# Two graph layers on one core: the filter's first products of two quads issued as a pair, projection and filter 2 in one PSUM bank

## Chip, cores and metric

The kernel runs on one core of one Trainium2 chip. The metric is device time in microseconds (us); before the change the median of three runs is 1879.74 us (1878.91 to 1882.81).

## What is computed

50,000 nodes and 50,000 edges, 128 channels, f32 in and out. A SchNet-like layer (senders `src`, receivers `dst`) is followed by a layer with a mean over neighbours (gather by `dst`, sum by `src`); each has a layer norm and a relu in front. The edges are sorted by `dst`. Cut to what matters:

```python
h = relu(layernorm(x))                                   # per node
basis = exp(-coef * (edge_weight[:, None] - centers)**2) # 50 centres per edge
ef = (softplus(basis @ Wf1 + bf1) - LOG2) @ Wf2 + bf2    # the filter, per edge
messages = (h @ W_lin.T)[src] * ef
agg = segment_sum(messages, dst)
x = x + (softplus(agg @ Wm1 + bm1) - LOG2) @ Wm2 + bm2
h = relu(layernorm(x))
neigh = h[dst] @ W_neigh.T + b_neigh
x = x + h @ W_self.T + b_self + segment_sum(neigh, src) / clip(count, 1)
```

## The kernel before, in words

The rows are handled in quads of 512 (four tiles of 128), 98 of them. The program has three parts: a sorting part (counts and ranks of the indices), one long software-pipelined part, and a final part that sums rows by bins (L1262 and around it). The change touches only the middle part.

The middle part is a sequence of steps s = 0 to 115, written out by `over_steps`: every engine runs its own `step(s, ...)`, and in step s it works on quads of several ages: quad s at the front of the pipeline, quad s-18 at its end. `there(q)` leaves out quads that don't exist. Order on one engine is program order; between engines there are semaphores that count quads (`pe.wait_ge(e_hT, s - 2 + 1)` waits until hT of quad s-2 is written). Most buffers exist once, some twice.

On the edge side a quad passes through these stations. GpSimd gathers its `x` rows (L787). VectorE takes row statistics (L819, L826), ScalarE and VectorE make the inverse root between them, ScalarE normalises (`norm_relu`, L1021, output xn). TensorE transposes xn into turn_ps (`turn`, L1097), ScalarE copies it out as hT, and TensorE multiplies it by wlin into proj_ps (`product`, L1091: the projection). Beside this, ScalarE makes the basis of two quads at a time (`make_basis`, L989 and L993, in even steps): partitions 0 to 49 hold that of the even quad, partitions 64 to 113 that of the odd one. TensorE multiplies one of the halves by wf1 into u_ps (`filter_up`, L1104), ScalarE and VectorE form the softplus (`clamp` L998, `exponential` L1002, `logarithm` L1007, `soften` L859; the result is su), and TensorE multiplies su by wf2 into filt_ps (L1091, after a bias product L1089: filter 2). ScalarE copies this out as efs (`evacuate`, L1027; the trace calls it efb), and VectorE multiplies proj_ps by efs (`message`, L870, counted by e_msg).

On the node side TensorE sums message windows (`block_sums`, L1113, 12 products of 64 rows in alternating halves of the array), ScalarE copies the sums out (aggs), TensorE multiplies by wm1 (L1150, into nu_ps) and later by wm2 ("mlp"), VectorE adds the residual (L897), normalises (L890), TensorE transposes (L1097 with comb), ScalarE copies out nhT, and TensorE forms `self` (wself) and `neigh` (wneigh). `hidden_out` (L1033) is ScalarE's copy of `neigh` to h1s; it waits for n_neigh. `edge_rows` (L1125) gathers rows of a stored h1 by one-hot products, and `rows_out` (L1040) copies them out.

What sets the order of the work is the text of each engine's step. Before the change TensorE's step s is: self(s-11), block_sums(s-8), mlp(s-9), edge_rows(s-17), wm1(s-8), filter_up(s), neigh(s-11), transpose of nxn(s-10), projection(s-2), filter 2(s-1), transpose of xn(s-1). ScalarE's step s is: aggs(s-9), hT(s-3), efs(s-3), norm_relu(s-2), clamp(s-9), rows_out(s-18), hidden_out(s-12), nhT(s-11), small logarithms and roots, exponential and logarithm (s-9), clamp and exponential (s-1), in even steps make_basis, logarithm(s-1). VectorE's step s is: one_hots(s-8), edge_hots(s-17), message(s-3), small work and soften(s-9), node_out(s-11), small work, node_norm(s-10), soften(s-1), residual(s-9), row statistics.

Of PSUM's eight banks the middle part names u_ps (0), turn_ps (1), proj_ps (2), filt_ps (3), two banks of tiles (4, 5), nu_ps (6) and node_ps (7).

Of the kernel before, what the change touches and what calls it, by code (L numbers as in the profile page):

```python
# [17 lines left out]
BASIS = 50  # L18
BASIS_AT = (0, 64)
# [132 lines left out]
def gnn_kernel(nc, ins, out_dram):  # L152
# [5 lines left out]
    with ExitStack() as ctx:  # L158
# [456 lines left out]
        with nc.If(unfit == 0), ExitStack() as fast:  # L615
# [9 lines left out]
            with ExitStack() as sems:  # L625
# [37 lines left out]
                x_keys, x_win, scattered = sa2("x_keys"), sa2("x_win"), sa2("scattered")  # L663
                x_hot, x_sum, x_src, x_pos, x_rows = sa("x_hot"), sa("x_sum"), sa("x_src"), sa("x_pos"), sa("x_rows")
                x_ones = sa("x_ones")
                u_ps, turn_ps, proj_ps, filt_ps, _, _, nu_ps, node_ps = bank
                self_ps = mlp_ps = neigh_ps = node_ps
                agg_at, rows_at = 0, 2 * P

# [143 lines left out]
                def _(dve):  # L813
# [106 lines left out]
                    def step(s, even, odd, pair, slot, late):  # L920
                        if there(s - 8):
                            one_hots(s - 8, even)
                        if there(s - 17):
                            edge_hots(s - 17, odd)
                        if there(s - 3):
                            message(s - 3, odd)
                        if there(s - 10):
                            square_root(s - 10, nroot, nsquare, n_root, n_square)
                        if there(s - 1):
                            square_root(s - 1, root[:], square[:], e_root, e_square)  # L930
                        if there(s - 10):
                            times_var(s - 10, nmv, nsquare, nratio, n_square, n_ratio)
                        if there(s - 2):
                            dst_column(s - 2, even)
                        if there(s - 1):
                            times_var(s - 1, emv[:, odd, :, :], square[:], ratio[:], e_square, e_ratio)
                        if there(s - 9):
                            soften(s - 9, nu_ps[:], bm1_low, nlu[:], nsu[:], n_softln, n_mlp, n_soft)
                        if there(s - 10):
                            correction(s - 10, nratio, nfactor, n_ratio, n_factor)  # L940
                        if there(s - 1):
                            correction(s - 1, ratio[:], factor[:], e_ratio, e_factor)
                        if there(s - 11):
                            node_out(s - 11, odd, late)
                        if there(s - 17):
                            row_keys(s - 17, odd)
                        if there(s - 1):
                            inverse_root(s - 1, factor[:], root[:], rstd[:], e_factor, e_norm, e_rstd)
                        if there(s - 10):
                            inverse_root(s - 10, nfactor, nroot, nrstd, n_factor, None, n_rstd)  # L950
                        if there(s - 7):
                            window_dst(s - 7, odd)
                        if there(s - 10):
                            node_norm(s - 10, even)
                        if there(s - 1):
                            mean_shift(s - 1, emv[:, odd, :, :], rstd[:], shift[:], e_rstd, e_shift)
                            soften(s - 1, u_ps[:], bf1_low, ln_out[:], su[:], e_softln, e_filter, e_soft)
                        if there(s - 9):
                            residual(s - 9, odd)
                        if there(s):  # L960
                            dve.wait_ge(gathered[even], half_count(s, even, 64))
                            row_stats(xg[:, even, :, :], stats, e_stats)
                            if there(s + 2):
                                take_src(s + 2, even)
                        if there(s - 9):
                            dve.wait_ge(n_x1, s - 9 + 1)
                            row_stats(x1[:, odd, :, :], nstats, n_stats)
                        if there(s):
                            wait_used(dve, e_ln, s, 2)
                            row_aggr(s, stats, emv[:, even, :, :], e_stats, e_aggr)  # L970
                        if there(s - 9):

                            wait_used(dve, n_ln, s - 9, 1)
                            row_aggr(s - 9, nstats, nmv, n_stats, n_aggr)
# [7 lines left out]
                def _(act):  # L982
# [58 lines left out]

                    nc.scalar.preload_act_table_set("natural_log_exp_and_others")
                    def step(s, even, odd, pair, slot, late):
                        if there(s - 9):
                            evacuate(s - 9, by_half(aggs[:]), tiles_ps(agg_at), n_agg, n_u, n_aggT)
                        if there(s - 3):
                            evacuate(s - 3, hT[:], turn_ps[:], e_turned, e_proj, e_hT)
                            evacuate(s - 3, efs[:], filt_ps[:], e_filter, e_msg, e_filter_sb)
                        if there(s - 2):
                            act.wait_ge(e_shift, s - 2 + 1)  # L1050
                            wait_used(act, e_turned, s - 2, 1)
                            norm_relu(xg[:, even, :, :], rstd, shift, xn, e_norm)
# [18 lines left out]
                        if there(s - 9):  # L1071
                            logarithm(s - 9, neu[:], nlu[:], n_exp, n_soft, n_softln)
                        if there(s - 1):
                            clamp(s - 1, u_ps[:], bf1_top, clampu[:], e_u, e_clamp)
                            exponential(s - 1, clampu[:], eu[:], e_clamp, e_exp)
                        if even == 0 and there(s):
                            make_basis(pair, slot)
# [5 lines left out]
                def _(pe):  # L1083
# [13 lines left out]
                            last = nc.tensor.transpose(turn_ps[:, t * P:(t + 1) * P], source[:, t, :], ident[:])  # L1097
                        last.then_inc(done, 1)

                    def filter_up(q, par, pair, slot):  # L1100
                        pe.wait_ge(basis_ready, pair + 1)
                        wait_used(pe, e_soft, q, 1)
                        at = BASIS_AT[par]
                        nc.tensor.matmul(u_ps[:], wf1[at:at + BASIS, :], basis[at:at + BASIS, slot, :], start=True, stop=True).then_inc(e_u, 1)  # L1104

                    def block_sums(j, par):
                        pe.wait_ge(n_hot, j + 1)
# [21 lines left out]
                    def step(s, even, odd, pair, slot, late):  # L1129
# [5 lines left out]
                        if there(s - 8):  # L1135
                            if there(s - 18):
                                pe.wait_ge(x_rows, s - 18 + 1)
                            block_sums(s - 8, even)
                        if there(s - 9):
                            if there(s - 11):  # L1140
                                pe.wait_ge(n_y, s - 11 + 1)
# [5 lines left out]
                        if there(s - 8):  # L1147
                            pe.wait_ge(n_aggT, s - 8 + 1)
                            wait_used(pe, n_soft, s - 8, 1)
                            nc.tensor.matmul(nu_ps[:], wm1[:], aggs[:], start=True, stop=True).then_inc(n_u, 1)  # L1150
                        if there(s):
                            filter_up(s, even, pair, slot)
                        if there(s - 11):
                            pe.wait_ge(n_y, s - 11 + 1)
                            if there(s - 9):
# [2 lines left out]
                        if there(s - 10):  # L1158
# [3 lines left out]
                                pe.wait_ge(e_hT, s - 2 + 1)  # L1162
                            wait_used(pe, n_hT, s - 10, 1)
                            turn(nxn, n_turned)
                        if there(s - 2):
                            product(s - 2, proj_ps, hT, wlin, None, e_hT, e_msg, e_proj)
                        if there(s - 1):
                            product(s - 1, filt_ps, su, wf2, 0, e_soft, e_filter_sb, e_filter)
                            pe.wait_ge(e_norm, s - 1 + 1)

# [990 lines left out]
```

## Time and profile before

| what | value |
|---|---|
| median of 3 runs | 1879.74 us (1878.91 to 1882.81) |
| profiled execution, its own time | 1883.8 us |
| its span in the profile | 1882.0 us |
| TensorE busy | 1690.9 us, 90% |
| VectorE busy | 1418.4 us, 75% |
| ScalarE busy | 1133.3 us, 60% |
| GpSimd busy | 1119.4 us, 59% |
| mean granted TensorE clock | 0.947 |

The profile shows one execution. The busy time of an engine is the union of its instructions' times, so that overlapping matmuls count once; of a matmul the end is modelled, so the distance from one group's start to the next one's is the safer measure of what it costs. An f32 product shows as two matmul records, each with its weight load: four products of 128 columns are "x8". In a timeline a row gives the start in us from the start of the span, the duration in us, engine, line, operation, names and shapes, and in brackets how long the engine sat idle before and who ended that. An instruction's start already has its semaphore waits behind it.

### The profile page before, as it was taken

How to read it: one execution, taken by the hardware profiler on the slowest of the kernel's cores; microseconds unless marked ns; L12 is line 12 of the kernel's file. 1: busy time of each engine (PE TensorE's matmuls, PEld its weight loads, DVE VectorE, ACT ScalarE, POOL GpSimd, SP SyncE). 2: the span in 40 equal slices, each digit the busy share in tenths (PEclk: the TensorE clock that was granted, in tenths of full speed). 3: DMA queues.
4: the chain of work that ended last, by engine and by line, in shares of the span. 5: the costliest groups of instructions: out<-in, count | busy, mean ns of one | idle time of the engine just before them, and what ended most of it. 6: DMA issues, size and time to landing. Idle time of an engine off the chain costs nothing. (4 is left out here: it accounts for less than half of the span.)

```text
span 1882.0 us, 49986 instructions
## 1 busy us (share of the span) xinstructions
PE 1690.9 (90%) x13254; PEld 1271.4 (68%) x13254; DVE 1418.4 (75%) x4622; ACT 1133.3 (60%) x2713; POOL 1119.4 (59%) x938
## 2 busy tenths in 40 slices
PE   2659679999999999999999999999999738888997
PEld 1223256777777777777777777777777628888897
DVE  8989647877787778777877777777777517777886
ACT  1007678877777777777777777777774303333333
POOL 5980144366666666666666666666653545566675
PEclk8769769999999999999999999999999859999999
DMA  2000035667777777777777766666666538999886
GB/s 81 0 0 1 23 94 141 177 202 209 217 211 206 207 212 215 207 206 213 212 204 206 208 196 185 187 193 190 184 177 184 144 107 254 265 272 269 244 224 171
DMA packets 293579, 333.96 MB, mean 177 GB/s; under 512 B 42220, under 2 KB 233710, under 8 KB 293486
## 3 DMA queue, kind: packets, MB, share of 16 engines
q1 hardware_dynamic: 216654, 255.35, 47.1%
q0 software_dynamic: 25088, 51.83, 10.0%
q10 hardware_dynamic: 51744, 25.70, 4.6%
q8 instruction: 39, 0.64, 0.2%
q14 instruction: 54, 0.44, 0.1%
HBM read 212.96 MB, written 119.75 MB: 177 GB/s over the span
## 5 line engine op out<-in xcount | busy, mean ns | idle before, releaser
L787 POOL DMA_INDIRECT xg<-in_x,srcs x392 | 418.6, 1068 | 423.4 <-issue 348.5
L798 POOL DMA_INDIRECT row_table<-row_out,posq x392 | 384.4, 981 | 174.3 <-issue 113.2
L1262 PE MATMUL psum<-bin_rows,bin_hot 128*128 128x129 f32 x2352 | 288.9, 281 | 53.7 <-DVE bin_hot L1235 53.5
L1262 PEld LDWEIGHTS psum<-bin_rows,bin_hot 128*128 128x128 f32 x2352 | 273.0, 193 | 69.7 <-DVE bin_hot L1235 40.3
L1235 DVE TENSOR_TENSOR bin_hot<-iota,bin_rel 128x1536 f32<-128x1536 f32 x98 | 176.6, 1802 | 5.3
L1125 PE MATMUL psum<-hwin,hotT 64*128 64x128 f32 x2352 | 166.5, 291 | 14.3 <-DMA hwin<-h_table 11.2
L870 DVE TENSOR_TENSOR msgw<-psum,efb 128x512 f32<-128x512 f32 x98 | 67.7, 691 | 147.2 <-PE psum L1091 117.9
L1125 PEld LDWEIGHTS psum<-hwin,hotT 64*128 64x128 f32 x2352 | 147.2, 197 | 26.9 <-issue 9.4
L1113 PE MATMUL psum<-hot,win 64*128 64x128 f32 x2352 | 159.3, 282 | 2.4 <-DVE hot L882 2.4
L1021 ACT ACTIVATE xn<-xg,shift,rstd 128x128 f32<-128x128 f32 x392 | 161.0, 494 | 0.0
L1089 PE MATMUL psum<-bias,ones 3*128 3x512 bf16 x392 | 152.1, 388 | 7.9 <-ACT h1s L1033 6.4
L1113 PEld LDWEIGHTS psum<-hot,win 64*128 64x128 f32 x2352 | 140.4, 189 | 14.6 <-DVE hot L882 2.6
L1104 PE MATMUL psum<-basis,wf 50*128 50x512 f32 x196 | 115.6, 671 | 25.8 <-DVE su L859 19.6
L1277 ACT ACTIVATE x<-psum,inverse 128x128 f32<-128x128 f32 x200 | 57.2, 368 | 128.6 <-DVE inverse L1245 128.6
L1033 ACT ACTIVATE h1s<-psum 128x512 f32<-128x512 f32 x98 | 58.6, 598 | 124.0 <-PE psum L1091 94.6
L569 ACT ACTIVATE psum<-psum,cols 128x196 f32<-128x196 f32 x130 | 51.1, 393 | 127.9 <-PE psum L544 127.9
L998 ACT ACTIVATE nclamp<-psum,cols 128x512 f32<-128x512 f32 x98 | 67.4, 688 | 94.8 <-PE psum L1150 94.0
L1089 PEld LDWEIGHTS psum<-bias,ones 3*128 3x128 bf16 x392 | 35.5, 91 | 122.9 <-issue 89.8
L1091 PE MATMUL psum<-wf,su 128*128 128x128 f32 x784 | 118.1, 296 | 0.0
L1277 ACT ACTIVATE nx<-psum,inverse 128x128 f32<-128x128 f32 x192 | 54.9, 369 | 102.2 <-DVE inverse L1245 102.2
L1091 PEld LDWEIGHTS psum<-wf,su 128*128 128x128 f32 x784 | 98.9, 198 | 23.3 <-issue 23.3
L1091 PE MATMUL psum<-wneigh,nhT 128*128 128x128 f32 x784 | 114.0, 288 | 0.0
(174 smaller groups left out, 3870.8 us busy)
## 6 DMA issues: line engine op xcount, KB each, us to landing
bin_rows<-row_table SPq DMA_DIRECT2D x196, 195.0 KB, 3.2
win<-msg_table SPq DMA_DIRECT2D x392, 96.8 KB
hwin<-h_table SPq DMA_DIRECT2D x392, 96.0 KB
msg_table<-msgw SPq DMA_DIRECT2D x98, 258.0 KB
nx<-in_x_nodes SPq DMA_DIRECT2D x98, 256.0 KB
h_table<-h1s SPq DMA_DIRECT2D x98, 256.0 KB
y_table<-ys SPq DMA_DIRECT2D x61, 256.0 KB
out<-xg ACTq DMA_DIRECT2D x50, 256.0 KB, 3.8
```

The source lines that it names most:

```text
L787: nc.gpsimd.indirect_dma_start(out=xg[:, par, t, :], out_offset=None, in_=ins["x"], in_offset=bass.IndirectOffsetOnAxis(ap=srcs[:, par, t: ...
L798: nc.gpsimd.indirect_dma_start(out=row_dram, out_offset=bass.IndirectOffsetOnAxis(ap=posq[:, par, t:t + 1], axis=0), in_=row_out[:, par, t ...
L870: nc.vector.tensor_tensor(msgw[:, par, :, 0:C], proj_ps[:].rearrange("p (t c) -> p t c", t=QT), efs[:].rearrange("p (t c) -> p t c", t=QT) ...
L1021: last = nc.scalar.activation(out[:, t, :], source[:, t, :], ACT.Relu, bias=shift_[:, t:t + 1], scale=rstd_[:, t:t + 1])
L1089: nc.tensor.matmul(ps[:], ones3[0:3, :], bias3[0:3, b, :], start=True, stop=False)
L1091: last = nc.tensor.matmul(ps[:, t * P:(t + 1) * P], left[:, t * P:(t + 1) * P], weights_[:], start=(b is None), stop=(b is None or t == QT ...
L1104: nc.tensor.matmul(u_ps[:], wf1[at:at + BASIS, :], basis[at:at + BASIS, slot, :], start=True, stop=True).then_inc(e_u, 1)
L1113: last = nc.tensor.matmul(tile_ps(agg_at, 2 * g + h), win[half_of(h), par, g, w, 0:C], hot[half_of(h), par, g, w, :], start=(w == 0), stop ...
L1125: last = nc.tensor.matmul(tile_ps(rows_at, 2 * g + h), hotT[half_of(h), par, g, w, :], hwin[half_of(h), par, g, w, :], start=(w == 0), sto ...
L1235: nc.vector.tensor_tensor(bin_hot[:, par, :, :, :], iota4[:].rearrange("p (b n) -> p b n", b=2).unsqueeze(2).broadcast_to([P, 2, BTILES, B ...
L1262: last = nc.tensor.matmul(bank[2 * slot + b][:, h * MW:(h + 1) * MW], bin_hot[:, slot % 2, b, w, h * P:(h + 1) * P], bin_rows[:, slot, b, ...
L1277: last = nc.scalar.activation(of_slot(means, slot)[:, t, :], sums_of(slot)[:, t // 2, t % 2, 0:C], ACT.Identity, scale=inverse[:, slot, t ...
```

## The change

`filter_up` is called in even steps only, and then issues the products of both quads of the pair, one behind the other: the even quad's from partitions 0 to 49 into bank 0, the odd one's from partitions 64 to 113 into bank 3. Filter 2 no longer has bank 3 and shares bank 2 with the projection. So TensorE's projection of quad s-2 moves from behind the nxn transpose to directly behind `block_sums`, and first waits until ScalarE has copied out filter 2 of the same quad; filter 2 of quad s-1 first waits for the message of quad s-2. On ScalarE the copies hT(s-3) and efs(s-3) move ahead of aggs(s-9).

```diff
-                u_ps, turn_ps, proj_ps, filt_ps, _, _, nu_ps, node_ps = bank
+                u_even, turn_ps, edge_ps, u_odd, _, _, nu_ps, node_ps = bank
+                u_of = (u_even, u_odd)
+                proj_ps = filt_ps = edge_ps
...
-                            soften(s - 1, u_ps[:], bf1_low, ln_out[:], su[:], e_softln, e_filter, e_soft)
+                            soften(s - 1, u_of[odd][:], bf1_low, ln_out[:], su[:], e_softln, e_filter, e_soft)
...
-                        if there(s - 9):
-                            evacuate(s - 9, by_half(aggs[:]), tiles_ps(agg_at), n_agg, n_u, n_aggT)
                         if there(s - 3):
                             evacuate(s - 3, hT[:], turn_ps[:], e_turned, e_proj, e_hT)
                             evacuate(s - 3, efs[:], filt_ps[:], e_filter, e_msg, e_filter_sb)
+                        if there(s - 9):
+                            evacuate(s - 9, by_half(aggs[:]), tiles_ps(agg_at), n_agg, n_u, n_aggT)
...
-                            clamp(s - 1, u_ps[:], bf1_top, clampu[:], e_u, e_clamp)
+                            clamp(s - 1, u_of[odd][:], bf1_top, clampu[:], e_u, e_clamp)
...
-                    def filter_up(q, par, pair, slot):
+                    def filter_up(q, pair, slot):
+
                         pe.wait_ge(basis_ready, pair + 1)
                         wait_used(pe, e_soft, q, 1)
-                        at = BASIS_AT[par]
-                        nc.tensor.matmul(u_ps[:], wf1[at:at + BASIS, :], basis[at:at + BASIS, slot, :], start=True, stop=True).then_inc(e_u, 1)
+                        for par, at in enumerate(BASIS_AT):
+                            nc.tensor.matmul(u_of[par][:], wf1[at:at + BASIS, :], basis[at:at + BASIS, slot, :], start=True, stop=True).then_inc(e_u, 1)
...
                             block_sums(s - 8, even)
+                        if there(s - 2):
+                            pe.wait_ge(e_filter_sb, s - 2 + 1)
+                            product(s - 2, proj_ps, hT, wlin, None, e_hT, e_msg, e_proj)
...
-                        if there(s):
-                            filter_up(s, even, pair, slot)
+                        if even == 0 and there(s):
+                            filter_up(s, pair, slot)
...
-                        if there(s - 2):
-                            product(s - 2, proj_ps, hT, wlin, None, e_hT, e_msg, e_proj)
                         if there(s - 1):
+                            wait_used(pe, e_msg, s - 1, 1)
                             product(s - 1, filt_ps, su, wf2, 0, e_soft, e_filter_sb, e_filter)
```

On TensorE, one step of the middle part, from block_sums (hot, win) to the transpose of xn. Before, every step reads:

```order
L1113 MATMUL psum<-hot,win 128x128 x12
L1089 MATMUL psum<-bias,ones 128x512
L1091 MATMUL psum<-wm,nsu 128x128 x4
L1125 MATMUL psum<-hwin,hotT 128x128 x12
L1150 MATMUL psum<-aggs,wm 128x512
L1104 MATMUL psum<-basis,wf 128x512
L1089 MATMUL psum<-bias,ones 128x512
L1091 MATMUL psum<-wneigh,nhT 128x128 x4
L1097 MATMUL psum<-ident,comb 128x128 x4
L1091 MATMUL psum<-wlin,hT 128x128 x4
L1089 MATMUL psum<-bias,ones 128x512
L1091 MATMUL psum<-wf,su 128x128 x4
```

Now an even step reads as below; an odd step is the same without the row of the basis (L1107).

```order
L1116 MATMUL psum<-hot,win 128x128 x12
L1093 MATMUL psum<-wlin,hT 128x128 x4
L1091 MATMUL psum<-bias,ones 128x512
L1093 MATMUL psum<-wm,nsu 128x128 x4
L1128 MATMUL psum<-hwin,hotT 128x128 x12
L1156 MATMUL psum<-aggs,wm 128x512
L1107 MATMUL psum<-basis,wf 128x512 x2
L1091 MATMUL psum<-bias,ones 128x512
L1093 MATMUL psum<-wneigh,nhT 128x128 x4
L1099 MATMUL psum<-ident,comb 128x128 x4
L1091 MATMUL psum<-bias,ones 128x512
L1093 MATMUL psum<-wf,su 128x128 x4
```

The projection (wlin, hT) stands four products earlier, ahead of mlp, edge_rows, wm1 and neigh, and the basis product is there twice in one step and not in the next.

On ScalarE, the end of one step and the start of the next. Before (lu is the logarithm of the edge side):

```order
L1007 ACTIVATE lu<-eu,cols 128x512
L1025 REGISTER_ALU
L1027 ACTIVATE aggs<-psum 128x2x2x128
L1027 ACTIVATE hT<-psum 128x512
L1027 ACTIVATE efb<-psum 128x512
L1021 ACTIVATE xn<-xg,shift,rstd 128x128 x4
```

Now:

```order
L1009 ACTIVATE lu<-eu,cols 128x512
L1029 ACTIVATE hT<-psum 128x512
L1029 ACTIVATE efb<-psum 128x512
L1027 REGISTER_ALU
L1029 ACTIVATE aggs<-psum 128x2x2x128
L1023 ACTIVATE xn<-xg,shift,rstd 128x128 x4
```

The copy of filter 2 (efb) is now the second behind the logarithm, where it was the third.

## Rows read from the trace of the kernel before

**Rows 1.** The page: its first line and the engines' busy time

```profile
span 1882.0 us, 49986 instructions
PE 1690.9 (90%) x13254; PEld 1271.4 (68%) x13254; DVE 1418.4 (75%) x4622; ACT 1133.3 (60%) x2713; POOL 1119.4 (59%) x938
```

**Rows 2.** Two stretches: length, busy PE PEld DVE ACT POOL, clock, DMA share, GB/s

```profile
500.00:600.00 100.00, 100.00 (x832) 75.03 (x832) 78.05 (x327) 77.31 (x168) 66.19 (x64) 1.00 0.73 210
1600.00:1700.00 100.00, 86.67 (x703) 81.82 (x701) 74.95 (x117) 33.16 (x116) 61.76 (x30) 0.98 0.93 269
```

**Rows 3.** Timeline of TensorE, one step and what leads into it

```profile
804.24 0.60 PE L1097 MATMUL psum<-ident,comb 128*128 128x128 f32 x4
804.68 1.06 PE L1091 MATMUL psum<-wlin,hT 128*128 128x128 f32 x8
805.67 0.38 PE L1089 MATMUL psum<-bias,ones 3*128 3x512 bf16 x1
...
806.98 0.60 PE L1097 MATMUL psum<-ident,xn 128*128 128x128 f32 x4
807.51 0.39 PE L1089 MATMUL psum<-bias,ones 3*128 3x512 bf16 x1
...
808.91 1.61 PE L1113 MATMUL psum<-hot,win 64*128 64x128 f32 x24
810.45 0.38 PE L1089 MATMUL psum<-bias,ones 3*128 3x512 bf16 x1
...
811.86 1.61 PE L1125 MATMUL psum<-hwin,hotT 64*128 64x128 f32 x24
813.39 1.13 PE L1150 MATMUL psum<-aggs,wm 128*128 128x512 f32 x2
814.45 1.12 PE L1104 MATMUL psum<-basis,wf 50*128 50x512 f32 x2
815.50 0.39 PE L1089 MATMUL psum<-bias,ones 3*128 3x512 bf16 x1
...
816.82 0.60 PE L1097 MATMUL psum<-ident,comb 128*128 128x128 f32 x4
```

**Rows 4.** Timeline of ScalarE, an odd step's and an even step's second half

```profile
804.52 0.60 ACT L1033 ACTIVATE h1s<-psum 128x512 f32<-128x512 f32 x1 [1.36 <-PE psum L1091]
...
808.75 0.72 ACT L1007 ACTIVATE lu<-eu,cols 128x512 f32<-128x512 f32 x1
...
817.10 0.60 ACT L1033 ACTIVATE h1s<-psum 128x512 f32<-128x512 f32 x1 [1.36 <-PE psum L1091]
...
822.02 0.63 ACT L993 ACTIVATE basis<-junk 128x512 f32<-128x512 f32 x1
822.55 0.71 ACT L1007 ACTIVATE lu<-eu,cols 128x512 f32<-128x512 f32 x1
823.17 0.58 ACT L1027 ACTIVATE aggs<-psum 128x512 f32<-128x512 f32 x1
823.64 0.59 ACT L1027 ACTIVATE hT<-psum 128x512 f32<-128x512 f32 x1
```

**Rows 5.** Timeline of all engines where TensorE waits for a ScalarE copy

```profile
289.01 0.60 ACT L1027 ACTIVATE aggs<-psum 128x512 f32<-128x512 f32 x1 [1.86 <-PE psum L1113]
...
289.66 1.12 PE L1150 MATMUL psum<-aggs,wm 128*128 128x512 f32 x2 [0.70 <-ACT aggs L1027]
```

**Rows 6.** Timeline of VectorE, from the residual to the message

```profile
812.02 0.69 DVE L897 TENSOR_TENSOR x<-psum,nx 128x512 f32<-128x512 f32 x1
...
816.01 0.95 DVE L910 TENSOR_TENSOR hotT<-dst_keys,reach 128x768 f32<-128x768 int32 x1
818.35 0.69 DVE L870 TENSOR_TENSOR msgw<-psum,efb 128x512 f32<-128x512 f32 x1 [1.39 <-PE psum L1091]
```

**Rows 7.** Line L1113, the first 80 ns of one block_sums: ns min/median/max, starts

```profile
L1113 PE MATMUL psum<-hot,win x2: 373/373/373, 821.5 to 821.5; 64*128 64x128 f32 x2
```

**Rows 8.** Timeline of TensorE behind a longer idle time, early in the middle part

```profile
304.94 2.93 PE L1113 MATMUL psum<-hot,win 64*128 64x128 f32 x24 [2.38 <-DVE hot L882]
```

## The prediction
> **What bounds the kernel now.** I read the page first, then the busy times by stretch, then the timeline of one step, engine by engine. The page shows TensorE busy for 1690.9 of 1882.0 us, far ahead of VectorE, ScalarE and GpSimd [rows 1]. By stretch it is plainer: in the middle part TensorE is busy for 100.00 of 100 us at a granted clock of 1.00, while VectorE has 78 and ScalarE 77 [rows 2]. The timeline of a step shows that nothing stands between TensorE's groups: from the transpose at 804.24 to the same one at 816.82 is 12.58 us, filled without an idle bracket [rows 3]. So a step lasts as long as TensorE's work, and every wait on TensorE is met early. The reader should note how early: ScalarE's copy h1s starts 0.28 us behind the neigh product (804.24 to 804.52, and 816.82 to 817.10) after having sat idle for 1.36 us [rows 3, 4]. ScalarE's second half step is therefore tied to TensorE's neigh product, and what comes behind it can't be early.
>
> **Part 1, the pair.** A basis product takes 1.05 us (814.45 to 815.50), and an odd step no longer has one; what an even step pays for two is not in this trace. From below: 1.05, if the halves run at once. From above: 2.11, one behind the other. The nearest row is block_sums, the same kind of product in alternating halves: 24 matmul records in 1.54 us (808.91 to 810.45), 0.064 each, where full-height ones, as the eight of the projection, take 0.99 us, 0.124 each [rows 3]. The first two records both start at 821.5 [rows 7]. So the halves overlap fully there, and I take 1.05 for the pair. If TensorE stayed the bound, this would save 1.05 us in two steps.
>
> Here a rule speaks against the row. The Trainium skill (TensorE: Matmul & The Clock Gate, Packing small matmuls) says that matmuls start and end strictly in program order. An f32 product is two records, so by that rule the second record of the even product would run beside the first of the odd one, and the pair would last three records, not two. With 0.53 us each that is 1.58 us, and the sum would be 1998 instead of 1975. The trace disagrees for block_sums, since both first records start together; the rule is kept as a rival below.
>
> **Part 2, the projection moved ahead, with a wait for efs.** It now stands behind block_sums of step s and waits for e_filter_sb of quad s-2. ScalarE makes that copy at the start of its step s+1, that is behind all of its step s; and its step s holds the copy h1s, which waits for neigh of TensorE's step s-1. This is a chain from the neigh product of one step to the projection of the next, and its length is in the rows. When ScalarE's step s is odd (no basis): neigh ends at 804.24, the logarithm lu starts at 808.75. The copy behind lu starts 0.62 later, the next one 0.47 after that, and ends 0.59 later (822.55, 823.17, 823.64, 824.23), so efs as second copy is done 1.68 us behind lu's start: 810.43, or 6.19 behind neigh [rows 3, 4]. When step s is even, the basis (its exponential at 822.02) lies in front of lu: neigh ends at 816.82, lu starts at 822.55, efs would be done at 824.23, 7.41 behind neigh. TensorE starts 0.05 us behind the end of a ScalarE copy (289.61 to 289.66) [rows 5]. So the projection starts no sooner than 6.24 us behind neigh in odd steps and 7.46 in even ones.
>
> TensorE itself gets there sooner. Between neigh and the new place of the projection lie: transpose 0.44, bias and filter 2 1.31 (805.67 to 806.98), transpose 0.53, bias and self 1.40 (807.51 to 808.91), block_sums 1.54; sum 5.22 [rows 3]. Before, the projection's 0.99 us lay there too, and nothing waited. Now TensorE idles 1.02 us in an odd step and 2.24 in an even one. Queued behind that wait is everything: mlp, edge_rows, wm1, neigh; and neigh is what releases ScalarE's next chain. The loop is closed.
>
> From the projection to the end of neigh: projection 0.99, bias and mlp 1.41 (810.45 to 811.86), edge_rows 1.53, wm1 1.06, bias and neigh 1.32 (815.50 to 816.82); sum 6.31, and 1.05 more in an even step for the pair [rows 3].
> An odd step lasts 6.24 + 6.31 = 12.55 us. An even step lasts 7.46 + 6.31 + 1.05 = 14.82 us. The two together are 27.37 us, against 25.16 before: 2.21 us more.
>
> **Part 3, filter 2 waits for the message.** VectorE's message of quad s-2 comes behind residual, statistics and one-hots of the mlp of the same step. From the end of mlp (811.86) the residual starts 0.16 later, the last one-hot at 816.01 and lasts 0.95, and the message takes 0.69: done 5.79 us behind mlp [rows 3, 6]. Filter 2 is reached 1.53 + 1.06 + 1.32 + 0.44 = 4.35 us behind mlp in an odd step, 5.40 in an even one. So TensorE waits up to 1.44 or 0.39 us here. This wait lies on TensorE's 5.22 us, which has 1.02 or 2.24 us to spare: 1.44 is followed by an even projection (2.24 spare), 0.39 by an odd one (1.02 spare). I cost it at nothing; its cover is the ScalarE chain, and without that chain it would be 1.83 us in two steps. VectorE's own wait for the projection (1.39 us idle before the message [rows 6]) goes; late next on VectorE is the mlp product.
>
> **Part 4, the rest.** aggs is copied one copy later than hT and efs; wm1 needs it 3.9 us behind the projection's start, and it is done 0.5 us behind it: nothing. Soften and clamp read another bank: nothing. The store of a message is issued on the SP queue behind its semaphore as before, and the messages come earlier: nothing. The second basis product reads what make_basis wrote for the pair anyway.
>
> **The sum.** The chain exists where neigh runs (from step 12) and edge quads are left (to step 97): 86 steps, 43 pairs. 43 x 2.21 = 95 us. Steps 0 to 11 wait for gathers and softens; I cost them at 0 with 5 us either way. The profiled execution's own time is 1883.8 us (span 1882.0); it becomes 1979. The runs' median is 4.1 us below that execution, so I predict 1975 us. A change of 0.2% is about what a measurement of this kernel can tell from none.
>
> **Rivals.**
> A, a dearer pair. If it lasts 1.58 us, every even step gets 0.53 longer: 43 x 0.53 = 23 us, 1998. If the halves don't overlap at all, 43 x 1.06 = 46 us, 2021. For both: each product here ends in a semaphore count of its own, block_sums only in one. Against: rows 7.
>
> B, faster: TensorE stays packed. If efs came within 5.22 us of neigh, and the message in time too, 49 pairs would save 1.05 us each, and the time would be 1828. The first of these is the point from which it decides: 5.22 us, against 6.24 and 7.46 in the rows; the sign turns at a mean chain of 5.75 us (6.24 and 7.46 sum to 13.70; less 2.21 and halved). For it: ScalarE is idle for a quarter of the time [rows 2]. Against: the idle time lies ahead of h1s, not behind it [rows 4], and B needs both waits away.
>
> C, the clock drops. Behind 2.38 us of idle, block_sums took 2.93 us instead of 1.61 [rows 8, 3]; the projection's wait in an even step (2.24 us less what filter 2 has already waited) stays below it, but another wait may join. If each even step paid those 1.3 us, 43 x 1.3 = 57 us more: 2032. Against: in the last part TensorE is busy 86.67 of 100 us and the clock is 0.98 [rows 2]; the changed pair of steps is busy for 24.1 of 27.4 us, 88%.
>
> D, only the message binds. If efs is in time and the message is not, two steps save 1.05 us and lose up to 1.83: 43 x 0.78 = 34 us, 1913; with a message path 0.4 us shorter per step it comes out as no change. Against: the same rows as B.
>
> **Numbers.** Forecast as summed: 0.62. Pair of three records: 0.13; no overlap: 0.05; C: 0.06; B: 0.07; D: 0.04; D with the shorter path, no change: 0.03. The range from 1945 to 2033 holds the forecast with each chain 0.3 us shorter or longer, the dearer pairs and the clock; it leaves out B and D, 0.14. Faster by over 0.2%: 0.07, within: 0.03, slower: 0.90.
>
> **What would show it.** The timeline should have steps of about 12.6 and 14.8 us in turn; the projection (L1093, wlin) with idle time in front released by the efb copy (L1029), in even steps more than in odd; block_sums directly ahead of it at 1.54 us; TensorE busy near 88% in the middle part at a clock near 1.00; the pair at 1.05 us from its start to the bias; VectorE's message with no wait for the projection; in some steps a short wait of filter 2 for the message. A middle part without idle brackets on TensorE, or efs copied less than 5.3 us behind neigh, would prove me wrong.

## The result, and the profile after

The changed kernel takes 1994.76 us (median of 4 runs, 1990.10 to 2003.58) against 1879.33 us before (4 runs, 1874.75 to 1882.81): ratio 1.0617, 95% interval 1.0594 to 1.0640. It is slower by 115 us. Forecast were 1975 us, slower, in a range from 1945 to 2033.

The page after, first line and busy times:

```profile
span 1991.7 us, 49992 instructions
PE 1664.8 (84%) x13254; PEld 1264.3 (63%) x13254; DVE 1407.3 (71%) x4622; ACT 1129.9 (57%) x2713; POOL 1112.4 (56%) x938
```

TensorE is busy for 26 us less than in [rows 1], and the span is 109.7 us longer. What was added is idle time, and the waits of TensorE after the change name it (total us, times, longest us):

```profile
PE psum L1093 <- ACT efb L1029: 77.2, 89, 2.8
PE psum L1091 <- DVE msgw L872: 70.1, 53, 3.6
```

The first is the projection waiting for the copy of filter 2 (efs), the second is filter 2 waiting for the message. Neither is in the profile before. The stretch that answers to the first of [rows 2] has the same clock and a TensorE that is no longer full:

```profile
500.00:600.00 100.00, 88.94 (x750) 67.07 (x749) 70.73 (x297) 70.41 (x156) 59.96 (x60) 1.00 0.65 189
```

The timeline of TensorE after, an odd step and an even one, answers to [rows 3]:

```profile
804.11 0.60 PE L1099 MATMUL psum<-ident,comb 128*128 128x128 f32 x4
...
807.89 1.61 PE L1116 MATMUL psum<-hot,win 64*128 64x128 f32 x24
810.36 1.16 PE L1093 MATMUL psum<-wlin,hT 128*128 128x128 f32 x8 [0.86 <-ACT efb L1029]
811.45 0.38 PE L1091 MATMUL psum<-bias,ones 3*128 3x512 bf16 x1
...
816.76 0.60 PE L1099 MATMUL psum<-ident,comb 128*128 128x128 f32 x4
818.82 0.37 PE L1091 MATMUL psum<-bias,ones 3*128 3x512 bf16 x1 [1.46 <-DVE msgw L872]
...
822.05 1.61 PE L1116 MATMUL psum<-hot,win 64*128 64x128 f32 x24
824.29 1.15 PE L1093 MATMUL psum<-wlin,hT 128*128 128x128 f32 x8 [0.64 <-ACT efb L1029]
...
829.38 1.13 PE L1107 MATMUL psum<-basis,wf 50*128 50x512 f32 x4
830.44 0.39 PE L1091 MATMUL psum<-bias,ones 3*128 3x512 bf16 x1
...
831.75 0.60 PE L1099 MATMUL psum<-ident,comb 128*128 128x128 f32 x4
```

From neigh's end (the start of the comb transpose, 804.11, 816.76) to the projection it is 6.25 us in the odd step and 7.53 in the even one; forecast were 6.24 and 7.46. Two steps take 27.64 us from 804.11 to 831.75, where they took 25.16. The pair costs 1.06 us (829.38 to 830.44) for four records. ScalarE in the same time answers to [rows 4]:

```profile
804.39 0.60 ACT L1035 ACTIVATE h1s<-psum 128x512 f32<-128x512 f32 x1 [1.37 <-PE psum L1093]
...
808.61 0.72 ACT L1009 ACTIVATE lu<-eu,cols 128x512 f32<-128x512 f32 x1
...
809.72 0.59 ACT L1029 ACTIVATE efb<-psum 128x512 f32<-128x512 f32 x1
...
817.04 0.60 ACT L1035 ACTIVATE h1s<-psum 128x512 f32<-128x512 f32 x1 [0.31 <-PE psum L1093]
...
822.49 0.70 ACT L1009 ACTIVATE lu<-eu,cols 128x512 f32<-128x512 f32 x1
...
823.58 0.59 ACT L1029 ACTIVATE efb<-psum 128x512 f32<-128x512 f32 x1
```

The reader should see the whole loop in these two fences: h1s starts 0.28 us behind neigh, efb ends at 810.31 and 824.17, and the projection starts 0.05 and 0.12 us behind it.

Where the 109.7 us lie can be read from landmarks, that is, from the same group of instructions in both traces. edge_rows starts for the first time in step 17, and that of step 98 is the first without edge quads at the front. Timeline of TensorE before:

```profile
327.22 1.61 PE L1113 MATMUL psum<-hot,win 64*128 64x128 f32 x24
...
384.36 1.61 PE L1125 MATMUL psum<-hwin,hotT 64*128 64x128 f32 x24
...
1402.80 1.61 PE L1125 MATMUL psum<-hwin,hotT 64*128 64x128 f32 x24
```

After:

```profile
332.93 1.61 PE L1116 MATMUL psum<-hot,win 64*128 64x128 f32 x24
...
399.05 1.61 PE L1128 MATMUL psum<-hwin,hotT 64*128 64x128 f32 x24
...
1514.69 1.61 PE L1128 MATMUL psum<-hwin,hotT 64*128 64x128 f32 x24
```

So 14.7 us were lost before step 17, 97.2 in the 81 steps from there (1115.6 instead of 1018.4, that is 13.77 instead of 12.57 a step), and what comes behind is 2.2 us shorter. In both ends 1.1 us is only the place of the landmark: after the change the projection stands ahead of edge_rows, before it stood behind. Taken at the start of block_sums, the loss before step 17 is 13.6 us, and 1.2 us come off behind step 98. The first line of each fence is block_sums of step 12: 5.7 of the 13.6 us are lost by there, and 7.9 in steps 12 to 16. In the first 5.7 there is a sorting part that, though unchanged, was 1.7 us shorter (the first basis product starts at 220.37 instead of 222.05), so steps 0 to 11 lost 7.4 us. A part of them looks like this on TensorE after the change:

```profile
303.40 0.60 PE L1091 MATMUL psum<-bias,ones 3*128 3x512 bf16 x1 [3.60 <-DVE msgw L872]
303.94 2.08 PE L1093 MATMUL psum<-wf,su 128*128 128x128 f32 x8
305.80 1.06 PE L1099 MATMUL psum<-ident,xn 128*128 128x128 f32 x4
306.79 2.58 PE L1116 MATMUL psum<-hot,win 64*128 64x128 f32 x24
```

Filter 2 waits 3.60 us for the message, and what follows runs at about half pace: 2.08 us where eight records take 1.16 at other times, 2.58 for block_sums instead of 1.61. The kernel before has waits and half pace in this stretch too [rows 8]: from 287 us to block_sums of step 12 its mean granted clock is 0.95, after the change 0.87. In steps 12 to 16, where edge_rows doesn't run yet, TensorE waits 1.6 to 1.7 us and 0.7 us for the message in turn and at most 0.2 us for efs.

### The profile page after: what moved, and what is told of

Same layout as the page of the kernel before. It is cut to its first block and busy times, and to the rows that moved or that the text cites. A ratio compares the mean times of both kernels' runs of the same rounds, so it can differ in the third digit from the quotient of the medians.

```text
span 1991.7 us, 49992 instructions
## 1 busy us (share of the span) xinstructions
PE 1664.8 (84%) x13254; PEld 1264.3 (63%) x13254; DVE 1407.3 (71%) x4622; ACT 1129.9 (57%) x2713; POOL 1112.4 (56%) x938
## 5 line engine op out<-in xcount | busy, mean ns | idle before, releaser
L789 POOL DMA_INDIRECT xg<-in_x,srcs x392 | 414.1, 1056 | 537.5 <-issue 393.6
L899 DVE TENSOR_TENSOR x<-psum,nx 128x512 f32<-128x512 f32 x98 | 67.8, 692 | 178.1 <-issue 170.8
L1093 PE MATMUL psum<-wlin,hT 128*128 128x128 f32 x784 | 117.1, 294 | 77.3 <-ACT efb L1029 77.2
L1093 PEld LDWEIGHTS psum<-wlin,hT 128*128 128x128 f32 x784 | 98.1, 196 | 96.6 <-ACT efb L1029 80.0
L1093 PE MATMUL psum<-wself,nhT 128*128 128x128 f32 x784 | 115.4, 291 | 0.0
L834 DVE TENSOR_TENSOR nsmall<-nsmall 128x4 f32<-128x4 f32 x98 | 16.0, 163 | 140.2 <-ACT nsmall L1019 138.2
```

The costliest lines, as they stand in the source:

```text
L789: nc.gpsimd.indirect_dma_start(out=xg[:, par, t, :], out_offset=None, in_=ins["x"], in_offset=bass.IndirectOffsetOnAxis(ap=srcs[:, par, t: ...
L899: nc.vector.tensor_tensor(flat(x1, par), mlp_ps[:], flat(nx, par), ALU.add).then_inc(n_x1, 1)
L1093: last = nc.tensor.matmul(ps[:, t * P:(t + 1) * P], left[:, t * P:(t + 1) * P], weights_[:], start=(b is None), stop=(b is None or t == QT ...
```

## The experiments

Theory 1 is the loop of the prediction: neigh, ScalarE's step from h1s to efs, projection, and back to neigh. The main rival was that filter 2's wait for the message sets the step. "Two steps" below is twice the mean step from edge_rows of step 17 to that of step 98, read from each run's timeline. The kernel before was measured again beside each version, with medians from 1875.84 to 1878.06 us, and the ratios are against that.

| kernel | us | ratio (95%) | two steps, us |
|---|---|---|---|
| before | 1879.33 | 1 | 25.15 |
| the change | 1994.76 | 1.0617 (1.0594 to 1.0640) | 27.55 |
| e1 projection behind edge_rows | 1919.59 | 1.0220 (1.0191 to 1.0249) | 25.90 |
| e2 and old order of copies | 1862.11 | 0.9914 (0.9890 to 0.9939) | 24.62 |
| e3 and message first | 1858.10 | 0.9896 (0.9871 to 0.9921) | 24.58 |
| e4 change, message first | 2085.06 | 1.1117 (1.1069 to 1.1165) | 29.82 |
| e5 change, old order of copies | 2141.53 | 1.1396 (1.1367 to 1.1426) | 30.71 |
| e7 change, basis behind the copies | 1962.01 | 1.0450 (1.0426 to 1.0474) | 26.67 |
| e8 = e3 and basis behind the copies | 1842.77 | 0.9813 (0.9793 to 0.9832) | 24.09 |
| e9 = e3, pair taken apart | 1908.10 | 1.0170 (1.0145 to 1.0196) | 25.64 |
| e10 change, projection in its old place | 1914.86 | 1.0210 (1.0184 to 1.0235) | 25.95 |

### e1: the projection behind edge_rows

The lines taken out stood behind block_sums.

```diff
-                        if there(s - 2):
-                            pe.wait_ge(e_filter_sb, s - 2 + 1)
-                            product(s - 2, proj_ps, hT, wlin, None, e_hT, e_msg, e_proj)
...
                             edge_rows(s - 17, odd)
+                        if there(s - 2):
+                            pe.wait_ge(e_filter_sb, s - 2 + 1)
+                            product(s - 2, proj_ps, hT, wlin, None, e_hT, e_msg, e_proj)
```

> The changed kernel with the projection of quad s-2 (and its wait for efs) moved from behind block_sums to behind edge_rows; ScalarE as in the change. Theory 1 (the loop neigh, ScalarE's step, efs, projection sets the step): the wait before the projection goes, since TensorE gets there 9.7 us behind neigh and efs is done after 6.3 or 7.5. What then ends last is ScalarE's aggs, now the third copy, which edge_rows waits for: 6.7 us behind neigh in an odd step, 8.0 in an even one, against 6.6 of TensorE's own work. From edge_rows to neigh 5.0 us, 6.05 with the pair: 11.7 and 14.05, together 25.8 us for two steps where the changed kernel has 27.6. 1905 to 1920 us. Rival (the wait of filter 2 for the message sets the step): the message needs the projection, which comes later now, so nothing is gained: 1990 us or more, and two steps at 27.6 or longer.

Measured: 1919.59 us, two steps 25.90. The wait for efs is gone from the full pipeline, and what ends last is what was named, in even steps (timeline of TensorE in e1):

```profile
814.48 1.61 PE L1128 MATMUL psum<-hwin,hotT 64*128 64x128 f32 x24 [1.44 <-ACT aggs L1029]
```

75 of the 115 us come back by moving one product by 2.9 us of TensorE's work. Theory 1 foretold the size, but the run doesn't rule the rival out, as it was meant to. The mlp product, on which VectorE's message follows, now stands ahead of the projection, so that the message comes earlier too: from neigh's end to the message's end it is 12.29 us in this even step (806.25 to 818.54) and 14.47 in that of the changed kernel (804.11 to 818.58), and filter 2's wait is gone with the other. Timeline of VectorE, the message in the changed kernel and in e1:

```profile
817.90 0.68 DVE L872 TENSOR_TENSOR msgw<-psum,efb 128x512 f32<-128x512 f32 x1
```

```profile
817.86 0.68 DVE L872 TENSOR_TENSOR msgw<-psum,efb 128x512 f32<-128x512 f32 x1
```

The two explanations are told apart by e4 and e7.

### e2: the old order of ScalarE's copies as well

```diff
+                        if there(s - 9):
+                            evacuate(s - 9, by_half(aggs[:]), tiles_ps(agg_at), n_agg, n_u, n_aggT)
                         if there(s - 3):
                             evacuate(s - 3, hT[:], turn_ps[:], e_turned, e_proj, e_hT)
                             evacuate(s - 3, efs[:], filt_ps[:], e_filter, e_msg, e_filter_sb)
-                        if there(s - 9):
-                            evacuate(s - 9, by_half(aggs[:]), tiles_ps(agg_at), n_agg, n_u, n_aggT)
```

> As the one before, and ScalarE's copies in the old order again (aggs, hT, efs). Theory 1: aggs is done 5.8 or 7.0 us behind neigh and no longer waited for, efs after 6.7 or 8.0, still ahead of the projection at 9.7. What is left is TensorE's work, 24.2 us for two steps with the pair, and up to 0.4 us of filter 2 waiting for the message: 24.6 us against 25.16 before the change, 43 times 0.56 = 24 us faster than before: 1845 to 1870. Rival (message): as in the run before, 1990 or more. Rival (the pair is worth nothing, its second product is paid elsewhere): not below 1880.

Measured: 1862.11 us, two steps 24.62. The pair and the shared bank are in this kernel, and it is faster than the kernel before the change. What cost 115 us is thus neither of them by itself. The gain on the kernel before is 0.9%, clear of noise but small.

### e3: the message ahead of the one-hots

```diff
+                        if there(s - 3):
+                            message(s - 3, odd)
                         if there(s - 8):
                             one_hots(s - 8, even)
                         if there(s - 17):
                             edge_hots(s - 17, odd)
-                        if there(s - 3):
-                            message(s - 3, odd)
```

> As the one before, and VectorE's message(s-3) ahead of the two one-hots of its step instead of behind them. Theory 1: the last 0.4 us of filter 2's wait go where aggs doesn't take their place, two steps at 24.2 to 24.6 us; and in the steps before the pipeline is full, where filter 2 waited up to 3.6 us behind one-hots that wait for windows, about 10 us come back. 1835 to 1855 us. Rival: if the message path already binds nothing, the same time as the run before within 3 us.

Measured: 1858.10 us, 3 us above the expected band and 4 us below e2, with overlapping intervals, so a gain by this edit isn't shown. In the full pipeline two steps are the same (24.58). edge_rows of step 17 starts at 383.28 instead of 385.75, so 2.5 us came back at the start where about 10 were expected. Timeline of TensorE, an even step: the message's wait went and aggs took its place.

```profile
813.84 1.61 PE L1128 MATMUL psum<-hwin,hotT 64*128 64x128 f32 x24 [0.47 <-ACT aggs L1029]
```

### e4: the changed kernel, with the message first and nothing else

The edit is that of e3 on the changed kernel.

> The changed kernel with nothing but VectorE's message(s-3) ahead of the two one-hots. It takes filter 2's wait for the message away and leaves the loop through efs. Theory 1: the 1.46 us of waiting before filter 2 in an odd step move to the projection, the two steps stay at 27.5 us; only the start of the pipeline gains some 10 us: 1980 to 1995. Rival (message): two steps get 1.4 us shorter, 43 times 1.4 = 60 us: 1930 to 1940.

Measured: 2085.06 us, far outside of both expectations. The waits behave as theory 1 says: in the full pipeline none is left before filter 2, and the projection's wait in even steps is 2.15 us, 1.5 more than in the change. But that is now one piece of idle time, and TensorE slows down behind it (timeline of TensorE in e4):

```profile
803.93 1.36 PE L1093 MATMUL psum<-wlin,hT 128*128 128x128 f32 x8 [2.15 <-ACT efb L1029]
...
807.77 2.93 PE L1128 MATMUL psum<-hwin,hotT 64*128 64x128 f32 x24
...
820.75 1.16 PE L1093 MATMUL psum<-wlin,hT 128*128 128x128 f32 x8 [0.86 <-ACT efb L1029]
```

edge_rows takes 2.93 us instead of 1.61, and some 8 us behind the gap the pace is that of 1.2 GHz. Late in the same run the same gap doesn't do it. An early and a late stretch show this (length, busy PE PEld DVE ACT POOL, clock, DMA share, GB/s):

```profile
500.00:600.00 100.00, 91.11 (x671) 67.72 (x670) 63.15 (x267) 59.09 (x129) 51.70 (x53) 0.88 0.58 169
1300.00:1400.00 100.00, 90.25 (x760) 68.36 (x759) 70.54 (x295) 70.09 (x156) 60.06 (x59) 1.00 0.59 170
```

In the second one the steps are 13.71 and 13.86 us, 27.57 for two: what theory 1 expects, and no gain from a message that comes earlier. So the loop through efs sets the length, and the rival is out. As a mean over the 81 steps, two steps take 29.82 us, 2.25 more than these 27.57; 40.5 times 2.25 is 91 us, and 90 are what e4 takes over the changed kernel. They come with the lower clock: the mean over the execution is 0.905, against 0.950 in the changed kernel.

### e5: the changed kernel with the old order of copies

The edit is that of e2 on the changed kernel.

> The changed kernel with ScalarE's copies in the old order (aggs, hT, efs), nothing else. Theory 1 (the loop neigh, ScalarE's step, efs, projection): efs is done one copy, 0.48 us, later in every step, so two steps go from 27.6 to 28.6 us: 43 times 0.96 = 41 us over the changed kernel, 2030 to 2045. The idle time ahead of the projection stays under 1.4 us, so the clock stays at 1.00. Rival (aggs or the message set the step): aggs comes earlier, the message no later: the same as the changed kernel or faster, at most 1997.

Measured: 2141.53 us, about 100 us over the expectation. The sign is right and the size isn't, because a link was missed. aggs is the first copy again, and it waits for block_sums, which stands directly ahead of the projection. hT and efs are queued behind it. So TensorE waits in every step for three copies that can't start before its own block_sums ends (timeline of TensorE):

```profile
800.90 1.16 PE L1093 MATMUL psum<-wlin,hT 128*128 128x128 f32 x8 [1.67 <-ACT efb L1029]
...
815.50 1.16 PE L1093 MATMUL psum<-wlin,hT 128*128 128x128 f32 x8 [1.75 <-ACT efb L1029]
...
823.94 0.37 PE L1091 MATMUL psum<-bias,ones 3*128 3x512 bf16 x1 [1.44 <-DVE msgw L872]
...
830.53 1.15 PE L1093 MATMUL psum<-wlin,hT 128*128 128x128 f32 x8 [1.75 <-ACT efb L1029]
```

From 800.90 to 830.53, at full pace, that is 29.63 us for two steps instead of the 28.6 expected. The mean of two steps is 30.71, and here the clock fell too, against the expectation: the granted clock is 0.91 in the stretch from 700 to 800 us, where the changed kernel has 1.00. Between the two profiled executions lie 151 us: some 84 by the waits at full pace, some 44 with the lower clock, and 23 outside of the 81 steps. Since the wait is now one for ScalarE's three copies behind block_sums, this run doesn't test the loop that starts at neigh. With the projection in its new place, ScalarE's new order is needed.

### e7: the basis out of the chain

```diff
                         if there(s - 9):
                             evacuate(s - 9, by_half(aggs[:]), tiles_ps(agg_at), n_agg, n_u, n_aggT)
+                        if even == 1 and there(s - 1):
+                            make_basis(pair, slot)
...
-                        if even == 0 and there(s):
-                            make_basis(pair, slot)
```

> The changed kernel with ScalarE's make_basis moved from ahead of the logarithm of an even step to behind the copies (hT, efs, aggs) at the start of the next step. The basis then isn't in the chain from neigh to efs, which is 6.25 us in even steps too instead of 7.53. Theory 1: the even projection is then set by TensorE's own path with the message wait of the odd step, 5.2 + 1.5 = 6.7 us; two steps go from 27.6 to 26.8, 43 times 0.85 = 36 us less: 1955 to 1965. Rival (the message alone sets the step): no change, 1990 to 2000.

Measured: 1962.01 us (1961.60 to 1962.20), two steps 26.67. This edit touches neither TensorE's order, the bank nor the message. It shortens ScalarE's part of the loop alone, and 33 us go, where the rival had no change (timeline of TensorE):

```profile
807.25 0.37 PE L1091 MATMUL psum<-bias,ones 3*128 3x512 bf16 x1 [1.47 <-DVE msgw L872]
...
812.02 1.16 PE L1093 MATMUL psum<-wlin,hT 128*128 128x128 f32 x8
...
825.73 1.16 PE L1093 MATMUL psum<-wlin,hT 128*128 128x128 f32 x8 [0.86 <-ACT efb L1029]
```

In even steps (812.02) the projection starts without a wait of its own: TensorE's own path with the message's 1.47 us is the longer one now, as expected.

### e8: the fastest version

The edit of e7 on e3.

> The fastest of the first four (projection behind edge_rows, old order of copies, message ahead of the one-hots) with make_basis behind the copies of the next step as well. There aggs ended last in even steps, 0.47 us of idle time ahead of edge_rows. Theory 1: that wait goes, TensorE is bound by its work again, two steps at 24.1 us instead of 24.6: 43 times 0.5 = 21 us off 1858: 1833 to 1842. Rival (the moved basis delays norm_relu and so the transpose or the gathers): not below 1855.

Measured: 1842.77 us (5 runs, 1840.81 to 1847.60), ratio 0.9813 with an interval from 0.9793 to 0.9832: some 35 us below the kernel before, and one microsecond above the expected band. TensorE is full again, as a stretch shows:

```profile
700.00:800.00 100.00, 100.00 (x873) 76.80 (x873) 80.50 (x344) 81.29 (x175) 69.02 (x67) 1.00 0.74 218
```

Two steps are 24.09 us, 1.06 less than before the change: one basis product.

### e9: the worth of the pair alone

On e3, `filter_up` is called in every step again, for one quad, each into its own bank:

```diff
-                        if even == 0 and there(s):
-                            filter_up(s, pair, slot)
+                        if there(s):
+                            filter_up(s, even, pair, slot)
```

> The same base as the one before, without the moved basis, and with the pair taken apart: one basis product in each step, as before the change, each into its own bank. Here TensorE is the bound, so that this is the worth of the pair alone. If the two products of the pair overlap fully (1.06 us for both in the trace), each odd step gets 1.05 us longer: 43 to 49 times 1.05 = 45 to 51 us over 1858: 1900 to 1912. If the pair had been worth only half, 1880 to 1885; nothing, 1858.

Measured: 1908.10 us, 50.0 us above e3 (the ratios to the kernel before are 1.0170 and 0.9896), and 1.06 us more for two steps. Here the second product of a pair is free. In the changed kernel its first two records start together as well (line L1107, 801.70 to 801.82: ns min/median/max, starts):

```profile
L1107 PE MATMUL psum<-basis,wf x2: 693/693/693, 801.7 to 801.7; 50*128 50x512 f32 x2
```

### e10: the shared bank without the move

The lines taken out stood behind block_sums; those put in stand directly ahead of filter 2.

```diff
-                        if there(s - 2):
-                            pe.wait_ge(e_filter_sb, s - 2 + 1)
-                            product(s - 2, proj_ps, hT, wlin, None, e_hT, e_msg, e_proj)
...
+                        if there(s - 2):
+                            pe.wait_ge(e_filter_sb, s - 2 + 1)
+                            product(s - 2, proj_ps, hT, wlin, None, e_hT, e_msg, e_proj)
                         if there(s - 1):
                             wait_used(pe, e_msg, s - 1, 1)
```

> The changed kernel with the projection back in its old place, directly ahead of filter 2, with which it shares the bank; pair and order of ScalarE's copies as in the change. It asks what the shared bank costs by itself, without the loop through efs. The projection finds efs long done. Filter 2 then waits for VectorE's message of the same quad: from the projection's end to the message's end was 0.79 us before the change (805.67 to 806.46), so TensorE idles about 0.83 us in each step. Theory 1 (the loop, and with it the place, is what cost 115 us): TensorE's own 24.1 us for two steps and two waits of 0.83, 25.8 us, 43 times 0.6 = 27 us over the kernel before: 1900 to 1912. Rival (sharing the bank is what costs, wherever the projection stands): 1980 or more.

Measured: 1914.86 us, 3 us above the band of theory 1 and far below the rival's 1980, two steps 25.95. Timeline of TensorE:

```profile
807.95 0.37 PE L1091 MATMUL psum<-bias,ones 3*128 3x512 bf16 x1 [0.97 <-DVE msgw L872]
...
821.37 0.39 PE L1091 MATMUL psum<-bias,ones 3*128 3x512 bf16 x1 [0.79 <-DVE msgw L872]
```

The waits are 0.97 and 0.79 us where 0.83 were expected. So the shared bank does need the projection to be moved, since next to filter 2 it costs more than the pair gives. It was moved to a place where it costs three times as much over the kernel before; behind edge_rows, in e8, it costs nothing that the timeline shows.

## Why the prediction was right

**Part 1, the pair.** Taken at 1.05 us from block_sums' rows, measured 1.06, and worth 1.06 us of two steps (e9). The rule of the Trainium skill (TensorE: Matmul & The Clock Gate, Packing small matmuls) that matmuls start in program order would, as the prediction applied it, have made it 1.58; the measured 1.06 us, and the first two records that start together, don't bear that out for these f32 products. Both dearer rivals of A fall.

**Part 2, the loop.** Right in mechanism, place and size. The chain from neigh to projection is 6.25 and 7.53 us (6.24 and 7.46 forecast). Shortening it (e7) brought 33 us where 36 were expected, and taking the message's wait away without touching it (e4, late stretch) brought nothing. e1 fits too, but would also fit the message; e5 meant to lengthen the loop and closed another one.

**Part 3, the message.** Forecast were up to 1.44 and 0.39 us of waiting, measured are 1.46, or 1.07 in every other pair of steps, and none; as said it costs nothing beside the loop in the full pipeline: when it is taken away (e4), the two steps at full clock stay at 27.57. What the prediction didn't say is that this wait has a use: it splits the idle time, and without it the clock falls (e4).

**The sum.** Forecast were 95 us on the profiled execution, and 109.7 came. Five terms account for the rest. First, two steps are 27.55 to 27.64 instead of 27.37: the projection now takes 1.09 us instead of 0.99 (810.36 to 811.45), in both steps, and the even chain is 0.07 longer. In 81 steps that makes 97.2 us instead of 89.5, 7.7 more. Second, the step that failed is "Steps 0 to 11 wait for gathers and softens; I cost them at 0 with 5 us either way": 7.4 us were lost there. Filter 2's wait for the message reaches 3.60 us, the projection's for efs is 1.0 to 2.8 us, and the mean clock is lower than before (0.87 to 0.95 from 287 us on); how the 7.4 us divide between these was not tried. Third, steps 12 to 16 were priced by the loop at 5.5 us and took 7.9, 2.4 more, since there the message is what TensorE waits for. Fourth and fifth, the sorting part was 1.7 us shorter and the part behind step 98 was 1.2 us shorter, where nothing was forecast. 95 + 7.7 + 7.4 + 2.4 - 1.7 - 1.2 is 109.6, which is the 109.7 within rounding.

The forecast time is 20 us below the measured one. 14.7 us of this are these terms; the other 5 are the way from the profiled execution to the median of the runs, which was put at 4.1 us less and came out at 1.0 us more (1993.79 to 1994.76).

**B and D** fell: efs was not in time. e8 shows the packed TensorE that B had in mind, at 24.09 us for two steps, with the projection 2.9 us later on TensorE and the copies, the basis and the message in another order.

**C** did not occur in the changed kernel's full pipeline (clock 1.00), but its mechanism is real: e4 has it at 90 us, with a single wait of 2.15 us instead of two of 1.46 and 0.64. C had 1.3 us for each even step; e4 pays about 3.1, since two steps take 30.7 us where the clock falls and 27.6 where it doesn't. That C didn't come true in the changed kernel was in part luck: the prediction leaned on a wait below the 2.38 us of [rows 8], and e4's 2.15 us is below that too.

## What to carry to other kernels

Before an operation is moved ahead on a full engine, measure the path to what it will wait for, along the other engine's program order, from the last thing that this engine itself releases there; if it is longer than the own work between the two, a loop closes and every round pays the difference. Here 6.25 and 7.53 us stood against 5.22, and the row that showed it was an idle bracket on the engine with time to spare. The two products in opposite halves of the array's rows were worth pairing here, and the bank that this takes was best shared between two products with microseconds of other work between them, so that each is read before the other comes. The same pair and the same shared bank made the kernel 6% slower or 2% faster, by the place of the projection together with what ScalarE and VectorE do first.

## What the runs showed of the hardware

Two f32 products of 512 columns in opposite halves of the array's rows, into two banks, take 1.06 us, where one alone takes 1.05, though each counts up a semaphore of its own.

TensorE's granted clock stayed at 1.00 with idle times of 1.46 and 0.64 us in one step and 0.86 in the next, and fell to a mean of 0.88 in the stretch from 500 to 600 us when the first two became one of 2.15; behind it TensorE ran at the pace of 1.2 GHz, the lower of its two levels, for about 8 us (edge_rows 2.93 us instead of 1.61). In e5, where two steps at full pace have waits of 1.67, 1.44 and 1.75 us, it was 0.91 from 700 to 800 us. Late in e4 the same 2.15 us left the clock at 1.00. What makes the difference between the two stretches was not tried and stays open.
